# Local attention beside a routed expert layer on one core: the division of the attention output moves from the middle of VectorE's step, two units back, to its beginning, three units back

## Time and profile before

| | before |
|---|---|
| median of three runs | 616.04 us |
| the profiled execution, its own time | 614.93 us |
| its span, first to last instruction | 613.1 us |
| TensorE matmuls, share of the span | 550.0 us, 90% |
| VectorE | 450.6 us, 73% |
| ScalarE | 240.7 us, 39% |
| GpSimd | 232.5 us, 38% |
| mean granted TensorE clock | 0.973 of full speed |
| chain that ended last | PE 60%, DVE 17%, DMA 6%, ACT 6%, issue 6%, POOL 4% |

### The profile page before, as it was taken

One profiled execution on the slowest core, in us unless ns is written; L12 is line 12 of the kernel. 1 busy time (PEld: TensorE's weight loads), 2 busy tenths in 40 slices (PEclk: granted clock), 3 DMA queues, 4 the chain that ended last, 5 costly groups with the idle time before them and its releaser, 6 DMA issues.

```text
span 613.1 us, 10368 instructions
## 1 busy us (share of the span) xinstructions
PE 550.0 (90%) x3302; PEld 475.3 (78%) x3302; DVE 450.6 (73%) x1045; ACT 240.7 (39%) x506; POOL 232.5 (38%) x172
## 2 busy tenths in 40 slices
PE   1989999979978999999999999999997978789945
PEld 1757899759857999898999898998886757678744
DVE  6777768998767567566567566468999799778984
ACT  1473553437352432523432523444343523243120
POOL 6133323248873232222232232223556653511430
PEclk9989999989999999999999999999998999879987
DMA  9525432113326677676567677543356545421220
GB/s 310 191 76 176 159 130 72 49 47 106 108 96 198 197 190 219 177 216 198 170 183 226 177 199 213 149 128 91 60 121 140 108 111 113 110 58 23 55 57 19
DMA packets 110442, 83.18 MB, mean 136 GB/s; under 512 B 42292, under 2 KB 108724, under 8 KB 110388
## 3 DMA queue, kind: packets, MB, share of 16 engines
q1 hardware_dynamic: 98628, 69.01, 38.2%
q0 software_dynamic: 6144, 8.39, 6.9%
q10 hardware_dynamic: 5616, 5.11, 2.4%
HBM read 59.41 MB, written 23.07 MB: 135 GB/s over the span
## 4 chain that ended last, share of the span: by engine, by line
PE 60%; DVE 17%; issue 6%; DMA 6%; ACT 6%; POOL 4%; SPq 1%; DVEq 0%; ACTq 0%
PE psV L946 12%; PE psM L996 11%; PE psS L921 8%; PE psM L1005 5%; PE psM L973 5%; DMA xnT<-ys_dram,slot 4%; PE psM L896 4%; PE psM L932 3%; DVE O L764 3%; PE psM L901 3%; PE psM L968 3%; DVE PTs L744 3%; PE psM L954 3%; DVE Sx L712 2%; ACT qBD L490 2%
## 5 line engine op out<-in xcount | busy, mean ns | idle before, releaser
L946 PE MATMUL psV<-VB,PTs 128*128 128x132 f32 x1024 | 135.3, 285 | 23.9 <-DVE O L764 23.9
L440 POOL TENSOR_TENSOR Sx<-Sx,mx 128x752 f32<-128x752 f32 x64 | 94.9, 1483 | 154.3 <-DVE mx L722 154.1
L946 PEld LDWEIGHTS psV<-VB,PTs 128*128 128x128 f32 x1024 | 129.6, 196 | 29.3 <-issue 28.2
L434 POOL TENSOR_TENSOR Sx<-Sx,cst 128x752 f32<-128x752 f32 x28 | 46.9, 1677 | 182.5 <-DVE Sx L712 182.5
L921 PE MATMUL psS<-kBD,qBD 128*128 128x188 f32 x512 | 99.3, 326 | 0.2 <-DVE Sx L712 0.2
L921 PEld LDWEIGHTS psS<-kBD,qBD 128*128 128x128 f32 x512 | 85.9, 192 | 9.4 <-issue 2.6
L744 DVE STREAM_TRANSPOSE PTs<-Sx 128x512 f32<-128x512 f32 x128 | 82.8, 685 | 4.2 <-ACT Sx L501 4.2
L712 DVE TENSOR_TENSOR Sx<-psS,cst 128x752 f32<-128x752 f32 x64 | 60.0, 938 | 30.3 <-PE psS L921 29.9
L996 PE MATMUL psM<-xT,EB 128*128 128x128 f32 x624 | 76.5, 276 | 1.6 <-DMA EB<-in_L_ffn_up_w 1.6
L764 DVE TENSOR_TENSOR O<-psV,rs 32x128 f32<-32x128 f32 x256 | 73.5, 287 | 4.8
L996 PEld LDWEIGHTS psM<-xT,EB 128*128 128x128 f32 x624 | 73.8, 192 | 4.0 <-issue 1.9
(11 more groups left out here) (106 smaller groups left out, 671.8 us busy)
## 6 DMA issues: line engine op xcount, KB each, us to landing
EB<-in_L_ffn_gate_w SPq DMA_DIRECT2D x39, 256.0 KB, 3.0
EB<-in_L_ffn_up_w SPq DMA_DIRECT2D x39, 256.0 KB, 3.6
EB<-in_L_ffn_down_w SPq DMA_DIRECT2D x39, 256.0 KB, 3.1
VB<-v_dram SPq DMA_DIRECT2D x256, 32.0 KB
stage<-xs_dram SPq DMA_DIRECT2D x39, 128.0 KB, 2.2
ys_dram<-yb ACTq DMA_DIRECT2D x39, 128.0 KB, 3.2
xs_dram<-blank SPq DMA_DIRECT2D x9, 512.0 KB, 3.1
v_dram<-vS SPq DMA_DIRECT2D x8, 512.0 KB, 3.0
```

The lines of the kernel that those rows point to most:

```text
L440: nc.gpsimd.tensor_tensor(s, s, mx[n % 3][:, :].unsqueeze(2).broadcast_to([P, 2 * G, KW]), ALU.subtract).then_inc(a_sub, 1)
L946: last = mm(psV[:, j, at:at + HS * VW], PTs[n % 2][:, k, j, i, :], VB[n % 2][:, i, k, :, VW * j:VW * j + VW], start=k == 0, stop=k == 1)
```

## The change

VectorE's step n now begins with `invert`, `divide` and `turned` of unit n - 3; before, the three stood in mid-step, for unit n - 2. `output(t)` and `attention(t)` follow in odd steps, 2t + 5, in place of even ones, 2t + 4; `result(c)` may come one step later (`4c + 7` in place of `4c + 6`, which matters for c = 12 to 15; for the others `C_STEP + 2 + c` is larger or the same); and the loops run one step longer.

```diff
-LAST = U + 2
+LAST = U + 3
...
-    if n >= 4 and n % 2 == 0 and (n - 4) // 2 < T:
-        found.append(("pr", (n - 4) // 2))
+    if n >= 5 and n % 2 == 1 and (n - 5) // 2 < T:
+        found.append(("pr", (n - 5) // 2))
...
-    return [c for c in range(NC) if max(C_STEP + 2 + c, 4 * c + 6) == n]
+    return [c for c in range(NC) if max(C_STEP + 2 + c, 4 * c + 7) == n]
...
             for n in range(LAST + 1):
+                if 0 <= n - 3 < U:
+                    invert(n - 3)
+                    divide(n - 3)
+                    turned(n - 3)
                 if n < U:
                     weigh(n)
...
-                if 0 <= n - 2 < U:
-                    invert(n - 2)
-                    divide(n - 2)
-                    turned(n - 2)
                 for i in pair_at(n, 1)[1:]:
```

## The result

The changed kernel takes **646.78 us**, the median of 4 runs (641.46 to 647.81), beside 615.71 for the kernel before (4 runs, 613.49 to 616.31): ratio **1.048 [1.0421, 1.0539]**. I had said 628 and 616 to 638. The direction is right, the size is not: the loss is 31 us, and I had worked out 12.8. The profiled execution took 641.46 us (span 639.6), at a mean granted clock of 0.963. Against the profiled execution of before, 614.93, it loses 26.5 us, and those are what the traces can account for. The executions of the changed kernel differ with the clock: those at 0.950 and 0.952 took 647.6 and 647.8.

The account below looks back on a forecast made before the run. TensorE was taken to bound the expert steps (18 to about 40), VectorE routing steps 8 to 10 and output steps from about 41. The terms summed to 12.8 us: 614.93 + 12.8 = 627.7, say 628; range 616 to 638.

Parts of the forecast that it names:

- The routing steps: Steps 8 to 10: three divisions instead of two ahead of GpSimd's run, +1.9 us; with the earlier steps, +0.1.
- the gain of 1.8 in steps 2 and 3: Steps 2 and 3: TensorE's wait for a bank goes or shrinks with the division out of the way, gaining 1.8 us.
- the price of the gate: `weighted` waits for the step-start division, delaying `sg` and `su`: 1.07 or 0.43 us per step wherever VectorE is the bound.
- The terms for steps 40 to 47 and 49 and 50: Output steps: +2.7 us for 40 to 47 (0.8 in step 40, 1.9 in 41 to 43), +1.5 for 49 and 50.
- the rival with the clock: Output steps: TensorE, held for divisions, drops to its lower clock; 9 us more, 637 in all; chance 0.20.
- the entry: Steps 18 and 19: projection now behind the wait for expert weights, 1.03 us, and TensorE about 0.2 later; +1.2 us.
- the tail: Step 56 to the end: later `weigh`, waits, gather 14, and an attention and result ahead of step 63's division; +4.9 us.
- GpSimd's cover: From `largest(10)`, GpSimd's queue of subtractions and scatters was to hide all other changes up to step 16.
- Step 48: Step 48: division of 1.9 us now stands behind VectorE's wait for the tanh, less 0.42 of attention moved out; +1.5 us.
- steps 52 to 55: Gathers and ScalarE bound up to step 54, where the added division equals the attention and result that left: 0.
- Absorbed: Rival: VectorE less tight, hiding each step's first term; only 4.6 us lost at the seams and end, 619.5; chance 0.17.
- the other side: Rival: the division fills VectorE's waits for `weighted` and costs nothing in several steps, a gain to 610; chance 0.06.

Follow-up runs that it names:

- the run with the filled steps: Changed kernel, with 26 spare TensorE matmuls ahead of `weighted` in steps 17, 43, 49, 50, 51 and 63: 638.13 us, ratio 1.0365.
- The run with 16 filled steps: Changed kernel, with 20 spare TensorE matmuls ahead of `weighted` in each of 16 steps: 639.33 us, ratio 1.0386.
- the run with the gate alone: Kernel before, division left in mid-step, `weighted` also waiting for a tiny VectorE memset at the start of the same step: 621.21 us, ratio 1.0082.
- The gate and the lost cover: Kernel before, with `weighted` also waiting for a step-start memset (621.21 us), or the division behind `ag` and `hTs` (624.29 us); both edits together 643.99 us.

## Why the prediction was right in direction and wrong in size

**What bounds the kernel** was read rightly. The experts lose nothing (W20 to W40: -1.4 us), and GpSimd's run starts at 130.85, 1.2 late. The routing steps cost that 1.2 where I had 0.1, since the gain of 1.8 in steps 2 and 3 was only 1.0 up to W4 (67.77 before, 67.09 after, from a start 0.27 later) and was gone by W8.

**The step that failed is the price of the gate: 1.07 us for a step with `sg`, 0.43 with `su`, "wherever VectorE is the bound".** The terms for steps 40 to 47 and 49 and 50 rest on it, and a part of the last. It was taken at 2.4 GHz throughout, and it is right where the clock stays there: 1.27 and 1.18 in steps 42 and 58, 0.41 in steps 41, 57 and 59. In steps 43 and 49 to 51 `weighted` ran in 3.4 to 3.7 us, and the waits were 1.7 to 2.7. Of the 7.1 us of steps 49 to 51 the run with the filled steps keeps 2.7, for the 1.5 of the forecast, which counted neither step 51 nor the attention that comes into odd steps; the other 4.4 are the low clock's. I had this as the rival with the clock and held against it that "the gaps between jobs are short, 1 to 2 us". They aren't. Nor is a short gap safe, and "a gap as long as the 4 to 7 us" misread the trace. In the stretch of before from 460 to 480, whose clock of 0.91 I cited, the slow `weighted` is this one, behind 1.90 us:

```profile
470.53 3.06 PE L946 MATMUL psV<-VB,PTs 128*128 128x132 f32 x16 [1.90 <-DVE O L764]
```

Another of before, at 535.79, took 3.86 us behind 0.99, and in the changed kernel one at 484.83 took 2.08 behind 3.50. The last gap alone doesn't tell which of them are slow.

I had taken the gaps from the kernel before, where TensorE runs a step ahead; the gate takes away that lead, as I wrote myself in the next paragraph, and a TensorE without a lead stands for all of VectorE's step that its own work doesn't fill, and in one piece: 5.52, 2.17 and 3.39 us above. It was in sight: steps 48 to 51 of before have 34.20 - 27.85 = 6.35 us in which TensorE is idle, and 3.55 us of VectorE's wait in step 48 come right ahead of the division that TensorE would have to wait for. The run with the filled steps shows both halves: 8.35 and 8.85 us where the clock is kept, 9.7 to 10.4 where not. On the direction the Trainium skill ("TensorE: Matmul & The Clock Gate", "What's actually happening"), that inactivity throttles and work releases, agrees with the traces (granted clock 0.58 behind the gap of 5.52 us, 1.00 where it was filled); what I left out was to apply it to the gaps that the change makes. The clock rival's own 9 us come near the 7 to 9 measured, but partly by luck: it had them in three of steps 41 to 43 and 57 to 59, and of these only 43 was hit. Its 637 misses 646.8, because it stands on the same forecast for the entry and the tail.

**Second, a victim was missed.** The gate term counted `sg` and `su`; the projection is behind `weighted` too, and VectorE's `attention` waited for it 16.7 us in place of 6.4. Little of that is in the output steps, 0.41 in step 45 and 0.35 in steps 57 and 59; 7.0 are in the tail. In an odd step it comes behind `hTs`, as here in step 45, which has no shared block and was put at 0:

```profile
471.87 1.45 POOL L440 TENSOR_TENSOR Sx<-Sx,mx 128x752 f32<-128x752 f32 x1 [1.97 <-DVE mx L722]
472.93 0.94 DVE L797 SCALAR_TENSOR_TENSOR xnT<-EB,xnT 128x512 f32<-128x512 f32 x1
473.47 1.82 POOL L450 DMA_INDIRECT xnT<-ys_dram,slot  x1
474.28 0.42 DVE L791 TENSOR_TENSOR X<-psM,cst 128x256 f32<-128x256 f32 x1 [0.41 <-PE psM L954]
```

Step 45 took 8.01 us for 6.86: 0.42 for the attention that has come into it (step 44, which it left, keeps its length, 7.25 us for 7.26), 0.41 for the projection, and 0.29 for a slower `silu` (0.94 us for 0.65; the last section has the reason), 1.12 of the 1.15.

**Third, the entry**, forecast at 1.2 for a wait for expert weights that didn't come (no DMA wait ahead of L996). 4.9 of the 6.0 us are in steps 16 and 17; I had put all up to step 16 under GpSimd's cover, and step 17 nowhere. In step 16 `ag` waits 4.08 us for the tanh, the division comes behind it, and after 4.62 us of gap on TensorE both `weighted` and `su` run slow.

```profile
178.72 0.69 DVE L780 SCALAR_TENSOR_TENSOR ag<-tg,psM 128x512 f32<-128x512 f32 x1 [4.08 <-ACT tg L517]
...
180.97 3.86 PE L946 MATMUL psV<-VB,PTs 128*128 128x132 f32 x16 [4.62 <-DVE O L764]
...
184.62 2.65 PE L973 MATMUL psM<-xnT,wsgu 128*128 128x512 f32 x4
...
187.32 0.69 DVE L785 SCALAR_TENSOR_TENSOR hTs<-ag,psM 128x512 f32<-128x512 f32 x1 [2.92 <-PE psM L973]
```

Here the two parts of the change both count: W20 is 4.9 us late with the division moved alone and 2.1 and 3.2 (two runs) with attention and results moved alone, but 0.5 early with only the results moved, so the odd steps of the attention, which I had taken to count only at the seams, seem to have a part in it. Which wait that is wasn't looked for.

**The tail** was 4.9 for 7.6 measured. From W63 to the end it took 25.7 us for 20.0, with the clock at 0.70 in both kernels, and with two slow `weighted` where before had one:

```profile
613.57 3.86 PE L946 MATMUL psV<-VB,PTs 128*128 128x132 f32 x16 [3.01 <-DVE O L764]
...
619.17 0.42 DVE L791 TENSOR_TENSOR X<-psM,cst 128x256 f32<-128x256 f32 x1 [2.18 <-PE psM L954]
...
622.67 3.49 PE L946 MATMUL psV<-VB,PTs 128*128 128x132 f32 x16 [3.54 <-DVE O L764]
```

The run with attention and results unmoved takes 21.9 for the same piece, so 3.8 of these 5.7 us go with the last attention and result, which stand ahead of the last divisions. The run with 16 filled steps, attention and results moved, takes 21.2 at a clock of 0.93, so 4.5 of the 5.7 go away with the clock kept. The two sums overlap, and the traces don't part them. Step 48 (+0.5 for 1.5) and steps 52 to 55 (-1.4 for 0) went a little better than forecast.

**The rivals.** The clock drop came on top of the forecast, as its rival had it. "Absorbed" and "the other side" did not happen; the run with the gate alone is the absorbed case, and what absorbs is the division in mid-step, which the change takes away. Most signs that I had named came: `weighted`'s wait over 40 (58.0), `rs` near 0 (3.3), about 1.1 and 0.4 us in steps 42 and 58 and in 41, 57 and 59, the experts unharmed. Missed were the waits in steps 43, 49 and 51 (1.7 to 2.0 for 0.4) and in step 50 (2.74 for 1.1), and the start of the experts, late by 7.2 and not by 1. The signs that came speak for the mechanism and not for its size; I had named no sign for the clock.

**Open.** The gate and the lost cover make 13.6 us more together than apart (12.9 in the profiled executions: 5.8 in steps 40 to 47, 6.9 in 49 to 51, 3.3 in 56 to 59, and all the rest together 3.1 less). Shown is that only together they give a row of slow `weighted` in steps 49 to 51, and that with the clock kept there these steps are 4.4 us shorter; how the rest divides between the clock elsewhere and the waits as such isn't told apart. Nor is why the moved attention and results gain 5 to 7 us with the division in mid-step and none with it at the head: in the profiled executions they bring W63 5.8 us forward there too and lose 3.8 in the tail, but the medians (641.8 without, 646.8 with) show no gain.

## What to carry to other kernels

An in-order engine's work that is moved from mid-step to the next step's head loses what it covered and holds back whatever waits for it; price the two together, since each alone may be nearly free (here 5.7 and 9.3 us apart, 28.6 together). Where a change takes away an engine's lead, work out its gaps in the new order, not in the old one. If new gaps open on TensorE, price what stands behind them at the slow row too: here 3.4 to 3.9 us for 2.08, behind gaps of 2.2 to 5.5 us, and in the kernel before behind 1.0 and 1.9 as well. And try the parts of a change alone: the seam that I had taken for a neutral part of this one is worth 1% by itself.

## What the hardware showed that I had not expected

GpSimd and VectorE hold each other up. I had priced only one side, the issues of the gathers. The other is the `silu` of VectorE (L797, both inputs in SBUF): in the changed kernel it takes 0.94 us in five places and 0.68 to 0.70 in the others. It is GpSimd's `subtract` (L440) that holds it, and not the gather. Each of the five starts 0.40 us before a `subtract` ends and ends 0.54 us behind its end, as in the rows of step 45 above, and the fifth has no gather beside it:

```profile
536.48 1.45 POOL L440 TENSOR_TENSOR Sx<-Sx,mx 128x752 f32<-128x752 f32 x1 [4.85 <-DVE mx L722]
537.53 0.94 DVE L797 SCALAR_TENSOR_TENSOR xnT<-EB,xnT 128x512 f32<-128x512 f32 x1
```

In the 14 traces of this case 24 `silu` start inside a `subtract` and take 0.74 to 0.95 us; the 200 others, 116 of them beside a gather's issue, take 0.65 to 0.72. The other way round, the issue of a gather takes 1.82 us in place of 1.55 where it starts 0.54 behind such a `silu`, 1.92 where it starts 0.19 behind a `result` operation (L807, 475.41), and in the kernel before 2.01 where it starts 0.09 behind one (L804, 464.36). Over the kernel that is (by line, busy us and mean ns) 1.5 us more for 14 `silu` and 0.7 for 28 issues:

```profile
L450 POOL DMA_INDIRECT xnT<-ys_dram,slot x28 | 45.0, 1607 | 14.1 <-ACT xnT L471 8.3 <-issue 4.3
L797 DVE SCALAR_TENSOR_TENSOR xnT<-EB,xnT 128x512 f32<-128x512 f32 x14 | 10.9, 780 | 7.0 <-ACT EB L546 7.0
```

Before, they were 44.3 and 9.4 us. The forecast had +0.9 us for the gathers and nothing for the `silu`. The Trainium skill ("SBUF — State Buffer", "SBUF: two separate sides") describes the ports that the two engines share as an exclusive lock, in both directions: whichever starts first has it for the whole instruction, and the other waits. The `silu` that ends 0.54 us behind `subtract` fits that. The issues don't in one direction: a gather's issue under way held up no `silu`.
